# Three projections of batch 1 ahead of the first attention pass, its other units at every second place

## The reference

```python
q = q * cos + _rotate_half(q) * sin
k = k * cos + _rotate_half(k) * sin
att = jnp.einsum('bhgqd,bhkd->bhgqk', qg, k) / math.sqrt(D_HEAD)
att = jnp.where(causal[None, None, None], att, -jnp.inf)
probs = jax.nn.softmax(att, axis=-1).astype(resid.dtype)
ctx = jnp.einsum('bhgqk,bhkd->bhgqd', probs, v)
...
x = x + _L0_attn_ref(_layernorm(x, axis=-1), L0_attn_Wq, L0_attn_Wk, L0_attn_Wv, L0_attn_Wo)
x = x + _L0_ffn_ref(_layernorm(x, axis=-1), L0_ffn_W_gate, L0_ffn_W_up, L0_ffn_W_down)
```

## Time and profile before

| | us |
|---|---|
| median of 3 runs | 767.51 (765.9 to 767.98) |
| the profiled execution | 768.28 |
| its span | 766.6 |
| TensorE busy | 741.2 |
| VectorE busy | 444.2 |
| ScalarE busy | 334.2 |
| GpSimd busy | 242.1 |

### The profile page before, as it was taken

One profiled execution on the slowest core, in us unless ns is written; L12 is line 12 of the kernel. 1 busy time (PEld: TensorE's weight loads), 2 busy tenths in 40 slices (PEclk: granted clock), 3 DMA queues, 4 the chain that ended last, 5 costly groups with the idle time before them and its releaser, 6 DMA issues.

```text
span 766.6 us, 12191 instructions
## 1 busy us (share of the span) xinstructions
PE 741.2 (97%) x4164; PEld 502.2 (66%) x4164; DVE 444.2 (58%) x1136; ACT 334.2 (44%) x646; POOL 242.1 (32%) x467
## 2 busy tenths in 40 slices
PE   5889999999999999999999999999999999999998
PEld 4644454544454443444788878888888888888886
DVE  6897789888987899998445433324232333231212
ACT  4337678767976788677333222111121111111111
POOL 4157786588658874566000000000000000000000
PEclk9969999999999999999999999999999999999999
DMA  7346369545334455531593003211014120030001
GB/s 274 87 120 193 116 190 286 161 127 162 108 109 119 147 175 157 165 101 43 161 292 108 28 14 130 85 59 45 15 55 137 38 71 27 0 110 1 1 0 56
DMA packets 74760, 81.86 MB, mean 107 GB/s; under 512 B 8865, under 2 KB 58529, under 8 KB 74497
## 3 DMA queue, kind: packets, MB, share of 16 engines
q1 hardware_dynamic: 73408, 79.98, 33.4%
q10 hardware_dynamic: 1296, 1.18, 0.5%
HBM read 57.02 MB, written 33.36 MB: 118 GB/s over the span
## 4 chain that ended last, share of the span: by engine, by line
PE 83%; DVE 9%; POOL 3%; ACT 2%; DMA 2%; issue 1%; SPq 0%; ACTq 0%; DVEq 0%
PE bank L1604 36%; PE ps_y L1658 15%; PE ps_o L1134 8%; PE ps_t L1256 7%; PE ps_s L1222 7%; PE ps_d L1174 6%; DVE ps_s L943 3%; PE ps_d L1195 2%; ACT probs L807 1%; PE bank L1643 1%; DVE m_raw L948 1%; POOL rot L611 1%; PE ps_s L1229 1%; DVE xt_lo L915 1%; DVE xn L910 1%
## 5 line engine op out<-in xcount | busy, mean ns | idle before, releaser
L943 DVE CUSTOM_DVE_ANT_0 ps_s<-ps_s,mask_row 128x512 f32<-128x512 f32 (+1 forms) x360 | 192.4, 583 | 35.5 <-PE ps_s L1222 32.9
L807 ACT ACTIVATE probs<-ps_t 128x512 f32<-128x512 f32 (+1 forms) x352 | 178.3, 559 | 65.6 <-PE ps_t L1256 65.2
L1561 DVE TENSOR_TENSOR h<-h,bank 128x512 f32<-128x512 f32 (+1 forms) x44 | 30.2, 687 | 215.3 <-PE bank L1604 215.3
L1222 PE MATMUL ps_s<-k_rows,q_rows 96*128 96x256 bf16 (+3 forms) x512 | 141.4, 310 | 4.8 <-DVE m_raw L943 2.7
L1256 PE MATMUL ps_t<-q_rows,k_rows 98*128 98x512 bf16 (+1 forms) x352 | 127.2, 365 | 1.8 <-ACT probs L807 1.4
L255 POOL TENSOR_TENSOR var_eps<-mean_var,eps 128x1 f32<-128x1 f32 x16 | 3.1, 191 | 279.1 <-DVE mean_var L250 279.1
L1499 ACT ACTIVATE h<-bank 128x512 f32<-128x512 f32 (+1 forms) x44 | 26.3, 598 | 146.6 <-PE bank L1604 146.3
L709 POOL TENSOR_SCALAR_AFFINE_SELECT probs<-probs 128x512 f32<-128x512 f32 x128 | 83.3, 650 | 0.0
L1134 PE MATMUL ps_o<-probs,v_ones 128*32 128x512 f32 (+3 forms) x1024 | 82.2, 438 | 0.2
L1507 ACT CAST h_hi<-h 128x512 fp32r<-128x512 f32 (+1 forms) x44 | 27.3, 620 | 126.1 <-DVE h L1561 126.1
L1222 PEld LDWEIGHTS ps_s<-k_rows,q_rows 96*128 96x128 bf16 x512 | 48.2, 100 | 47.2 <-DVE m_raw L943 21.2
(11 more groups left out here) (167 smaller groups left out, 1372.1 us busy)
## 6 DMA issues: line engine op xcount, KB each, us to landing
scratch_o<-o_sb SPq DMA_DIRECT2D x31, 256.0 KB, 2.0
q_rows<-scratch_q_parts SPq DMA_DIRECT2D x32, 192.0 KB
x_in<-in_x SPq DMA_DIRECT2D x16, 256.0 KB, 4.2
q_rows<-scratch_q_parts SPq DMA_DIRECT2D x32, 128.0 KB
o_in<-scratch_o SPq DMA_DIRECT2D x64, 64.0 KB
inverse<-scratch_inverse SPq DMA_DIRECT2D x64, 64.0 KB
x_res<-in_x SPq DMA_DIRECT2D x16, 256.0 KB, 2.7
out<-x_in SPq DMA_DIRECT2D x16, 256.0 KB, 2.1
```

The source lines that it names most:

```text
L807: nc.scalar.activation(probs[:, g % 2, heads * u:heads * (u + 1), CHUNK_AT[c]:CHUNK_AT[c + 1]], ps_t[:, pos % S_BANKS, 0:heads * CHUNK_N[c ...
L943: taken = nc.vector.tensor_tensor_reduce(out=head, in0=head, in1=mask_row[:, T - width:T], scale=1.0, scalar=LOWEST, op0=ALU.add, op1=ALU. ...
L1222: mm = nc.tensor.matmul(bank[:, place], q_rows[r][0:ROWS, j, P * q:P * (q + 1)], k_rows[r][0:ROWS, 0:width], start=(place == 0), stop=(mas ...
L1561: nc.vector.tensor_tensor(h[0:m, r], h[0:m, r], bank[units["up", f] % BANKS][0:m, :], ALU.mult).then_inc(h_ready, 1)
```

## The change

Three of the six projections of batch 1, the units "R" 0, 1 and 2 (the keys and half of the queries), leave pass 0. Their twelve pieces stand in the preamble between the plain scores of groups 0 and 1, at the places of the table `AHEAD_AT` (group, slot, head: unit, piece), in one bank each (`ps_t`, `ps_d`, and `ps_o`, which is free there). ScalarE copies the first of them out ahead of batch 0's last `rotated_top`, the other two behind the store of batch 0's last part. GpSimd does the first four steps of batch 1's rotation, the keys, ahead of pass 0. What remains in pass 0 begins earlier, with its pieces at every second place. Group 0's maxima are transposed to `ps_t` and not `ps_d`, with semaphores of their own. Passes 1 to 3 keep their order.

```diff
-    for place, (kind, k, first) in enumerate(units):
-        steps = [gap(first + n) for n in range(1 if kind in "TU" else 4)]
+    for place, (kind, k, first, *apart) in enumerate(units):
+        steps = [gap(first + n) for n in ((0,) if kind in "TU" else range(0, 4 * apart[0], apart[0]) if apart else range(4))]
...
+AHEAD = 3
+AHEAD_AT = {(0, 1, 1): (0, 0), (0, 1, 3): (0, 1), (0, 2, 1): (0, 2), (0, 2, 3): (0, 3),
...
+FIRST_UNITS = [("R", 3, 2, 2), ("R", 4, 11, 2), ("V", 0, 19, 2), ("U", 0, 27)]
+UNITS_IN = [FIRST_UNITS + NEXT_T] + [QKV_UNITS + NEXT_T] * (B - 3) + [QKV_UNITS, LAST_UNITS]
+PRE_DENSE = KC + N_ROPE + 2 + KC + AHEAD
...
+ROPE_AHEAD = 4
+FIRST_ROPE = [None] * ROPE_AHEAD + [1, 2, 3, 5, 6, 7, 9, 10, 13, 14, 15, 17, 18, 19, 21, 22]
...
+LO_SLOT = [{1: 0, 9: 1, 13: 2, 21: 3, 25: 4}] + [{7: 0, 13: 1, 16: 2, 23: 3, 27: 4}] * (B - 2)
...
+            for s in range(ROPE_AHEAD):
+                rotate(1, s)
+                if s in REST_STEP:
+                    rotated_low(1, REST_STEP.index(s))
...
             store_rotated(act, 0, 3)
+            raw_rows(1, 0, r_unit(1, 0))
             rotated_top(0, 4)
             first_max_high()
             max_evacuate(0)
             store_rotated(act, 0, 4)
+            for k in range(1, AHEAD):
+                raw_rows(1, k, r_unit(1, k))
...
-                    bank_free(PRE_UNITS - 1, 0)
-                    to, ready = ps_d[:], dense_ready
+                    pe.wait_ge(dense_evacuated, KC + N_ROPE + 2 + KC)
+                    to, ready = ps_t[:, 0], first_max_ready
...
                         scores(0, n, i, j)
+                        if (n, i, j) in AHEAD_AT:
+                            k, piece = AHEAD_AT[n, i, j]
+                            dense(1, "R", k, r_unit(1, k), piece)
```

More of the change, by code:

```diff
@@ L80 @@
               ("T", 3, 39)]
-UNITS_IN = [QKV_UNITS + NEXT_T] * (B - 2) + [QKV_UNITS, LAST_UNITS]
-PRE_DENSE = KC + N_ROPE + 2 + KC
-PRE_UNITS = PRE_DENSE + 1
+AHEAD = 3
+AHEAD_AT = {(0, 1, 1): (0, 0), (0, 1, 3): (0, 1), (0, 2, 1): (0, 2), (0, 2, 3): (0, 3),
+            (1, 0, 1): (1, 0), (1, 0, 3): (1, 1), (1, 1, 1): (1, 2), (1, 1, 3): (1, 3),
+            (1, 2, 1): (2, 0), (1, 2, 3): (2, 1), (1, 3, 1): (2, 2), (1, 3, 3): (2, 3)}
+FIRST_UNITS = [("R", 3, 2, 2), ("R", 4, 11, 2), ("V", 0, 19, 2), ("U", 0, 27)]
+UNITS_IN = [FIRST_UNITS + NEXT_T] + [QKV_UNITS + NEXT_T] * (B - 3) + [QKV_UNITS, LAST_UNITS]
+PRE_DENSE = KC + N_ROPE + 2 + KC + AHEAD
 PRE_BANKS = 1 + S_BANKS
-UNIT0 = [PRE_UNITS + sum(len(u) for u in UNITS_IN[:b]) for b in range(B)]
-ROPE_SLOT = [3, 4, 5, 6, 7, 8, 10, 10, 11, 12, 13, 14, 15, 17, 18, 19, 21, 22, 23, 25]
+UNIT0 = [PRE_DENSE + sum(len(u) for u in UNITS_IN[:b]) for b in range(B)]
+ROPE_AHEAD = 4
+FIRST_ROPE = [None] * ROPE_AHEAD + [1, 2, 3, 5, 6, 7, 9, 10, 13, 14, 15, 17, 18, 19, 21, 22]
+ROPE_SLOT = [FIRST_ROPE] + [[3, 4, 5, 6, 7, 8, 10, 10, 11, 12, 13, 14, 15, 17, 18, 19, 21, 22, 23, 25]] * (B - 2)
 KEY_STEPS, PAIR_STEPS = 4, 8
@@ L328, in dense_bank @@
         def dense_bank(unit):
-            if isinstance(unit, int) and unit < PRE_DENSE and unit % PRE_BANKS:
+            if unit == PRE_DENSE - 1:
+                return ps_o[:]
+            if unit < PRE_DENSE and unit % PRE_BANKS:
                 return ps_t[:, unit % PRE_BANKS - 1]
@@ L398, in w_unit, with v_unit @@
             return LAST_UNIT0 + t
+        def v_unit(b):
+            return UNIT0[b - 1] + len(UNITS_IN[b - 1]) - KC - 1 if 0 < b < B - 1 else UNIT0[b] - 1 if b else KC + N_ROPE + 1
         def r_unit(b, k):
-            return UNIT0[b - 1] + k if b else KC + k
+            if b == 0:
+                return KC + k
+            if b == 1:
+                return PRE_DENSE - AHEAD + k
+            return UNIT0[b - 1] + k
         def rest_done(engine, b, k):
@@ L540, in iteration @@
                         stage_max(n + 1)
-                    if has_next and slot - 2 in LO_SLOT:
-                        store_rotated(sp, b + 1, LO_SLOT[slot - 2])
+                    if has_next and slot - 2 in LO_SLOT[b]:
+                        store_rotated(sp, b + 1, LO_SLOT[b][slot - 2])
                     if i == PV_EVACUATE and n >= 1:
@@ L724, in iteration @@
                     if has_next:
-                        for s, at in enumerate(ROPE_SLOT):
+                        for s, at in enumerate(ROPE_SLOT[b]):
                             if at == slot:
@@ L795, in max_evacuate @@
                 if n == 0:
-                    act.wait_ge(dense_ready, PRE_UNITS)
-                    nc.scalar.copy(m_t[0][:], ps_d[rows, 0:P]).then_inc(dense_evacuated, 1)
+                    act.wait_ge(first_max_ready, 1)
+                    nc.scalar.copy(m_t[0][:], ps_t[rows, 0, 0:P]).then_inc(first_max_evacuated, 1)
                 else:
@@ L850, in iteration @@
                                 dense_read(b, *done[slot, j])
-                    if has_next and slot in LO_SLOT:
-                        rotated_top(b + 1, LO_SLOT[slot])
+                    if has_next and slot in LO_SLOT[b]:
+                        rotated_top(b + 1, LO_SLOT[b][slot])
                     if not has_next and (slot - CTX_HI) % TT == 0 and 0 <= slot - CTX_HI < TT * TT:
@@ L1013, in next_work @@
                     if slot in NEXT_XT:
-                        work.append(lambda: xt_low(b + 2, NEXT_XT[slot], UNIT0[b] + len(QKV_UNITS) + NEXT_XT[slot]))
+                        work.append(lambda: xt_low(b + 2, NEXT_XT[slot], UNIT0[b + 1] - KC + NEXT_XT[slot]))
                 return work
@@ L1128, in weighted_v @@
             if c == 0:
-                if positive(n):
+                if n == 0:
+                    pe.wait_ge(dense_evacuated, PRE_DENSE)
+                else:
                     pe.wait_ge(o_evacuated, n)
@@ L1251, in scores_t @@
                 pos = T_AT[c] + u
+                if n == 0 and c == 0 and j == 0:
+                    pe.wait_ge(dense_evacuated, PRE_DENSE - AHEAD + 1)
                 if c == 0 and j == 0:
@@ L1284, in tensor_engine @@
                         mm.then_inc(dense_ready, 1)
-            for unit in range(KC, PRE_DENSE):
+            for unit in range(KC, PRE_DENSE - AHEAD):
                 kind, k, of = ("R", unit - KC, 0) if unit < KC + N_ROPE else (
```

7 lines of the change are left out of this document (4 added, 3 removed).

## The result

The changed kernel takes 769.84 us (median of 17 runs, 767.64 to 771.68) against 767.37 (17 runs, 765.9 to 768.43) for the kernel before on the same chips. The ratio is 1.0032, interval 1.0021 to 1.0043: slower by 0.3%, or 2.5 us. The forecast was 2.7 us faster, and the time lies outside its range.

A forecast was written before the change was run, and what follows sets the result against it. TensorE was taken to set the pace, busy for 97% of the span. A shift of +3.4 us before pass 0 and a gain of 6.1 in it summed to -2.7, giving 764.8 us, with a range from 761.8 to 768.7.

The forecast's parts named there:

- part 2: Plain scores before pass 0: full clock back at 46.4 us (44.5 to 48.6), with no second low stretch.
- part 3: Group 0's maximum before pass 0: its cast waits behind ScalarE's copies, costing TensorE 1.3 us (0 to 2.5).
- part 7: Everything else, including first maximum's bank and DMA queue: costs nothing; first pass's stores merely come two to six slots earlier.
- parts 1 and 2: Plain scores before pass 0: 36 added matmuls cost 8.2 us at full clock; scores end at 57.9 (56.9 to 59.0).
- r: Moment the full clock returns in the plain scores before pass 0: between 44.5 and 48.6 us, taken as 46.4.
- part 6: GpSimd in pass 0: four rotation steps move ahead; its work fits the second and fifth stretches, 9.0 in 9.1, 8.7 in 9.4.
- Part 4: Start of pass 0: transpose of group 1's maxima at 60.9 instead of 57.52, shift +3.4 us (+1.2 to +5.7).
- the 62 named as the sign: Start of pass 0: forecast of the start is wrong if group 1's transpose stands past 62 us or before 59.5.
- Part 5: Pass 0's six stretches between maxima transposes: pieces taken out gain 6.1 us (4.3 to 7.4).
- the 9 to 9.6 named as the sign: Pass 0: transposes after group 1's should be 9 to 9.6 us apart up to the sixth stretch.
- the rival of the gain eaten: Pass 0: VectorE and GpSimd turn local waits, gain only 3.3 us against shift 3.4, so 767.6; chance 0.28.
- the slower one: Plain scores before pass 0: clock stays low; back at 60 us costs 6.8 more, 771.6; chance 0.12.

The follow-up runs named there:

- f_oldplaces: Changed kernel with ScalarE's copies after rounding and cast, last store back in its slot, and pass 0's remaining pieces, rotation steps and stores at old places: 766.08 us, ratio 0.9994.
- b_store: Changed kernel with batch 1's last rounding and store back at slots 27 and 29 instead of 25 and 27: 767.12 us, ratio 1.0004 to the kernel before.
- e_xslot: Changed kernel with ScalarE's copies after rounding and cast, last store back in its slot, and next input's load at slot 30 instead of 26: 764.47 us, ratio 0.9967.
- h_all: Changed kernel with ScalarE's reorder, last store back in its slot, batch 3's input loaded at slot 30, fourth projection one place earlier: 764.13 us, ratio 0.9955.
- d_fill: Changed kernel with six unused 512-column matmuls of constants ahead of the first maximum's transpose: 768.62 us, ratio 1.002 to the kernel before.
- after_again: The changed kernel unedited, run once more to look for the second clock fall: 769.96 us, ratio 1.0041 to the kernel before.
- a_order: Changed kernel with ScalarE's three projection copies moved behind batch 0's last rounding and the cast of group 0's maxima: 765.73 us, ratio 0.9983 to the kernel before.
- i_port: Changed kernel with GpSimd's first rotation product made to wait until VectorE has split group 0's maxima: 767.11 us, ratio 1.0004 to the kernel before.
- g_early: Changed kernel with ScalarE's copies after rounding and cast, last store back in its slot, and the fourth projection one place earlier: 764.37 us, ratio 0.9968.

## Why the prediction was wrong

It failed at part 2's sentence "I expect no second low stretch", at the size of part 3, and at part 7's "the DMA queue meets the same transfers". The first two belong together.

1. *Pieces put in, parts 1 and 2.* The way to add them up was right (though the middle of 44.5 and 48.6 is 46.55, not 46.4). The clock came back at 45.0, 4.5 us after the start of the plain scores; the forecast's 44.5 to 48.6 is 3.7 to 7.8. In the other profiles with the pieces put in it came back 1.2 (f_oldplaces) to 6.8 us (b_store) after that start. In e_xslot, f_oldplaces and h_all it took only 1.2 to 1.6, far outside the bounds, so that r fell inside them here is partly luck. The Trainium skill's remark, cited there, that the moment differs between executions ("TensorE: Matmul & The Clock Gate", Part 1) is borne out by this spread. But I had looked for waits only between short scores, and the wait that brought the clock down was in part 3's own chain: 1.2 and 0.6 us in a stream otherwise tight. The fall costs 1.56 us (d_fill, after_again), and came in all four of the changed kernel's profiles.

2. *Part 3, the late maximum: mechanism right, size wrong.* Cast at 51.24 (forecast 52), transpose at 52.77 (52.4), VectorE idle 1.22 ("1.5 or so"). The stall was to be 1.3, at most 2.5. Taking its cause away gains 3.8 to 4.1 (a_order): 1.4 to 1.6 for the cast (a_order against i_port), which is about the 1.3 charged, 1.0 for VectorE's subtraction being held by GpSimd's product, 1.56 for the clock (d_fill). I moved GpSimd's rotation to a new place in part 6 and asked only whether it had room there, not what VectorE does beside it.

3. *Part 4, the shift: +3.4 became +6.2, past its upper bound of 5.7.* The transpose stood at 63.71, past the 62 named as the sign. Without collision and fall, i_port takes 20.39 us from the first plain score to the transpose, +3.7 over before, so the rest of the sum was sized well.

4. *Part 5, the gains: 6.1 became 5.5.* By stretch, forecast and found: w0 0.5 and 0.0, w1 2.3 and 2.4, w2 1.5 and 1.9, w3 0.65 and 0.4, w4 0.85 and 0.7, w5 0.3 and 0.1. w1 to w4 lasted 8.7 to 9.9, a little wider than the 9 to 9.6 named as the sign, and w1's length is below the 9.6 that would have refuted it. The term that failed is w0. One piece fewer took nothing off it. The trace's reading is that slot 1 is then held by VectorE's maxima and ScalarE's exponentials: in b_store its part ahead of its piece lasts 1.96 us with both busy throughout and TensorE 1.76, and the whole slot 2.57 against 2.21 in the kernel before, with one piece in each. No run tests this by itself; g_early shows that a piece put into slot 0 is paid elsewhere.

5. *Part 7.* The stores were counted as "two to six slots earlier" and hidden. One of them landed in front of m_t in SyncE's queue: +1.14 us in w7. The order accounts for 0.58 (b_store). The other half goes when four loads leave the queue ahead of m_t (e_xslot); whether by its earlier issue or by emptier transfers stays open. This is the question "which queue is it moved past" that I did not ask of SyncE.

6. *The rivals.* None named either mechanism. The measured 769.84 lies between the rival of the gain eaten (767.6) and the slower one (771.6), a little nearer the second, but neither had the reason. In the first w1, w2 and w4 were to end at 9.9; they ended at 9.04, 8.73 and 9.53. The slower rival needed the clock to come back after 51.8; it came back at 45.0.

The sum with the measured sizes, for the profiled executions: 6.46 - 0.27 - 5.52 - 0.08 + 1.14 - 0.2 = +1.5. The medians differ by 2.5. The other 1.0 is mostly the kernel before's: its profiled execution (768.28) lay 0.9 above its median, the changed kernel's (769.84) on its own. The record points at the clock ahead of pass 0, though no second profile of that kernel shows it. In 79 later executions of the kernel before, the 31 with a mean granted clock of 0.989 or less have a median of 768.0, the 27 at 0.992 or more 766.1; the profiled one is at 0.988. And the four profiles of the changed kernel differ above all there: the first one's low stretch lasted from 34.8 to 45.1 and group 0's transpose stood at 52.77, the three others' was over by 42.1 to 42.7 (39.3 to 42.7 in after_again) and the transpose stood at 50.13 to 50.61. What decides in which executions the clock falls again was not found either: after a like wait it fell in four profiles and not in b_store's.

## What to carry to other kernels

When a stream is made dense to get the clock back, look for the one chain inside it that the added work delays (here a cast of 16 columns behind three copies): its wait costs itself and can bring a second low clock. For each step that moves, ask three things: what stands behind it in its queue, which other queue's hand-over it now passes, and which engine it runs beside. And fewer pieces help only if they are spread: here the same pieces closer together lose 2.3 of 5.5 us.

## What the hardware showed that was not expected

**A short VectorE instruction can last as long as GpSimd's.** The subtraction of two 16-column SBUF tiles took 1.22 us in the six profiles in which GpSimd's product (two SBUF inputs, 1.26 us) began 0.07 or 0.08 us earlier, and 0.17 or 0.18 in the eight others. i_port is one of these, and moved nothing but that product's start. The profile shows it as VectorE's busy time, not as a wait. The Trainium skill ("SBUF — State Buffer", "SBUF: two separate sides") calls the port pair that the two engines share "an exclusive lock, not a bandwidth split"; whichever starts first keeps it for the whole instruction; for VectorE it names instructions with two SBUF inputs, against a GpSimd one that reads SBUF. These rows agree.

**The clock can fall inside a busy stream.** Waits of 1.2 and 0.6 us, with work between them, were followed 1.3 us later by a fall to 1.2 GHz; without the 1.2 us wait (a_order, d_fill, i_port) there was none. It is not a fixed consequence: the same waits in b_store were not followed by a fall.

**A small load can take 3.6 to 5.4 us.** m_t, 32x128 bf16, took 3.59 us from issue to landing in the changed kernel and 5.35 in b_store, where a copy of weights (`in_wu`, issued at 122.87) and the stores of the rotation, issued from 127.79 on, were under way beside it. Which of them made it longer was not tested.
